# Cross-attention's sums by way of DRAM: one store, two loads and a wide reciprocal in place of ten transposes a pair

## The chip, the cores and the metric

One core of a Trainium2 chip. The metric is the device time of one execution in microseconds; the kernel before has a median of 562.46 us over three runs (562.35 to 567.57). The engines are TensorE (PE, with its weight loads as PEld), VectorE (DVE), ScalarE (ACT), GpSimd (POOL) and SyncE (SP), which issues nearly all DMAs.

## The reference

A decoder layer on x of (32, 64, 256), with context of the same shape. Each sublayer adds its result to x and is followed by a layer norm without gain.

```
x = layernorm(x + self_attention(x))          # 16 heads of 16, causal over 64 rows
x = layernorm(x + cross_attention(x, ctx))
x = layernorm(x + feed_forward(x))            # quantised 256 -> 1024 -> 256, silu, gelu, layer norm between
```

Cross-attention takes the 64 rows as channels and the 256 columns as positions: 8 heads of 8 channels.

```
q, k, v = heads(Wq x + bq), heads(Wk c + bk), heads(Wv c + bv)     # c: the context; q and k rotated
p   = softmax(q k^T / sqrt(8))                                     # 256 x 256 per head
out = Wo concat_heads(p v) + bo
```

## The kernel before

The 32 sequences are worked in 16 pairs; a pair's two sequences lie on 2 x 64 partitions. The first stage (`phase_a`) is a loop over bodies, -1 to 15. Body i works at once on several pairs: cross-attention's exponentials and products of pair i, the row maxima (`max_tile`) of the tiles 14 steps ahead, self-attention of pair i+3, and the end of cross-attention of pair i-1 (`prev`). Each engine runs a list written out by hand: a body has 16 steps `s`, and a line such as `if s == 13` says which piece stands after which step's tile. Engines meet by semaphores only. The maxima alternate between two PSUM banks, so TensorE's tile n waits for VectorE's reduction of tile n-2 (L574), and the exponentials do the same with ScalarE.

Cross-attention of a pair, per sequence b: `pv_quad` (L615) multiplies the exponentials by VA, whose 32 columns per head are 8 values and 24 ones. So u_b holds, on partition 32j + c and column 256 s4 + t, for c below 8 the weighted sum of value c of head 4 s4 + j at position t, and for c from 8 on copies of the sum of the exponentials. `u_copy` (L778) brings it to US of 128x512, after step 8 for b = 0 and after step 0 of the next body for b = 1. Then:

- `u_transpose` (L241): four 128x128 transposes on TensorE for each b, in step 13 and in step 3 of the next body;
- `u_norm` (L276): on VectorE a reciprocal of 16 sums a partition and a multiply, into AN;
- `att_transpose` (L250): two transposes back, in step 5; `at_copy` (L261) on ScalarE adds the value bias and writes AT;
- `x_out_proj` (L257) in step 9, `norm2_stats` (L291) in step 10, `rstd` on POOL, `norm2` in step 13.

SyncE's queue (`body` at L440) runs in order and each DMA waits for its data: `load_c`, `max_rows(i, 1)`, `cross_values`, `store_parts("q")`, `max_rows(nxt, 0)`, `expand_rows("q")`, `load_x`, `store_parts("k")`, `load_xT`, `expand_rows("k")`. `max_rows` (L405) puts the negated maxima into rows of QA, which the exponentials' product of steps 0 and 8 waits for; `expand_rows` (L379) reads the bf16 parts of q or k back from DRAM in copies.

A second program block follows: feed-forward in TURNS1 = 19 turns of the first product (`first_product`, `first_bias`), then 25 turns of the second stage. The last pair's end of cross-attention lies in its first turns: u_transpose ahead of turn 0, u_norm in turn 1, att_transpose in turn 2, x_out_proj in turn 3, norm2_stats in turn 4.

```
def max_ready(i, n):
    if has(i, 1) or n >= 2:
        pe.wait_ge(mx_red.sem, 16 * i.v + n - 1)
```

Of the kernel before, what the change touches and what calls it, by code (L numbers as in the profile page):

```python
# [80 lines left out]
def build_layer(nc, x, xT, ctx, wpT, woT, xW, xB, rows, w1T, w2T, attn_tables, rotary_tables, out):  # L81
    with ExitStack() as outer:
# [46 lines left out]
        RD = sb("RD", [P, 16])  # L129
        AN = sb("AN", [P, 2, 2, SEQ])  # L130
        AT = sb("AT", [P, D])
        Y2, st2, mv2, rs2 = sb("Y2", [P, D]), sb("st2", [P, 6]), sb("mv2", [P, 2]), sb("rs2", [P, 3])
# [4 lines left out]
        u_sb, ut_ps, u_nrm = event("u_sb", 2), event("ut_ps", 2), event("u_nrm", 4)  # L137
        at_ps, at_sb, xo_ps = event("at_ps"), event("at_sb"), event("xo_ps")
# [102 lines left out]
        def u_transpose(pe, i, b, ps):  # L241

            wait(pe, u_sb, i, b + 1)
            for u in range(2):
                for s4 in range(2):
                    q = 2 * u + s4
                    last = nc.tensor.transpose(ps[:, P * q:P * q + P], US[:, s4, P * u:P * u + P], ident)
            last.then_inc(ut_ps.sem, 1)

        def att_transpose(pe, i, ps):  # L250

            wait(pe, u_nrm, i, 4)
            for u in range(2):
                last = nc.tensor.transpose(ps[:, P * u:P * u + P], AN[:, u].rearrange("p b c -> p (b c)"), ident)
            last.then_inc(at_ps.sem, 1)

# [3 lines left out]

        def at_copy(act, i, g):  # L261
            wait(act, at_ps, i, 1)
            if has(i, 1):
                wait(act, xo_ps, i.plus(-1), 1)

            nc.scalar.activation(AT[:, :], g_b[g][:, 0:D], ACT.Identity, bias=xb["v"]).then_inc(at_sb.sem, 1)
# [9 lines left out]
        def u_norm(dve, i, b, g):  # L276
            wait(dve, ut_ps, i, b + 1)
            sums = g_b[g][:, :].rearrange("p (u h c) -> p u h c", u=2, c=32)
            if b == 1:
                wait(dve, u_nrm, i, 2)  # L280
            elif has(i, 1):
                wait(dve, u_nrm, i.plus(-1), 4)
                wait(dve, at_ps, i.plus(-1), 1)
            nc.vector.reciprocal(RD[:].rearrange("p (u h) -> p u h", u=2).unsqueeze(3),
                                 sums[:, :, :, XC:XC + 1]).then_inc(u_nrm.sem, 1)
            wait(dve, u_nrm, i, 2 * b + 1)
            nc.vector.tensor_tensor(AN[:, :, b, :].rearrange("p u (h c) -> p u h c", c=XC), sums[:, :, :, 0:XC],
                                    RD[:].rearrange("p (u h) -> p u h", u=2).unsqueeze(3).broadcast_to([P, 2, XH, XC]),
                                    ALU.mult).then_inc(u_nrm.sem, 1)

        def norm2_stats(dve, i, g):  # L291
            wait(dve, xo_ps, i, 1)
            if has(i, 1):
                wait(dve, ln2, i.plus(-1), 7)
            wait(dve, ln1, i, 7)
            nc.vector.scalar_tensor_tensor(out=Y2[:].unsqueeze(1), in0=g_b[g][:, 0:D].unsqueeze(1), scalar=xb["o"],
# [55 lines left out]
        def _(sp):  # L352
# [87 lines left out]
            def body(i):  # L440
                nxt, j, a = i.plus(1), i.plus(2), i.plus(3)
                if i.v >= 1 and real(a):
                    load_c(a)
                if real(i):
                    max_rows(i, 1)
                if real(a):
                    cross_values(a)
                if real(j):
                    store_parts("q", j)
                if real(nxt):  # L450
                    max_rows(nxt, 0)
                if real(j):
                    expand_rows("q", j)
# [9 lines left out]
                if real(a):  # L463
                    expand_rows("k", a)
# [841 lines left out]
        def _(dve):  # L1306
# [80 lines left out]
            for t in range(TURNS1):  # L1387
# [12 lines left out]
                if t == 9:  # L1400
                    factors(dve, 2)
# [71 lines left out]
```

## Time and profile before

| | |
|---|---|
| median of 3 runs | 562.46 us |
| the profiled execution | 563.8 us |
| its span, first to last instruction | 561.9 us |
| mean granted TensorE clock | 0.848 of full |
| busy: TensorE, VectorE, ScalarE, POOL | 450.6, 442.4, 382.0, 289.6 us |
| instructions | 12026 |

Times in the rows are microseconds from the span's start. "Busy" of an engine leaves out waits; a row's bracket gives the idle time before it and who ended it. A transfer's time to landing runs from its issue.

### The profile page before, as it was taken

What the parts mean: (1) busy time and instruction counts of PE and PEld (TensorE: products, weight loads), DVE (VectorE), ACT (ScalarE), POOL (GpSimd) and SP (SyncE); (2) the same over time, 40 slices, a digit from 0 to 9 for tenths busy, and PEclk for the clock granted to TensorE, in tenths of its full rate; (3) what the DMA queues carried; (4) which work ended last, traced back from release to release, by engine and by line L of the source; (5) the groups of instructions that cost most, each with busy time, mean ns of one, the idle gap of its engine ahead of it and who ended that gap; (6) DMA issues with size and microseconds to landing.
All of it is one profiled execution on the core that took longest, in us unless ns stands there. A gap on an engine that the chain in (4) does not pass through costs nothing. (4 is left out here: it accounts for less than half of the span.)

```text
span 561.9 us, 12026 instructions
## 1 busy us (share of the span) xinstructions
PE 450.6 (80%) x4162; PEld 243.0 (43%) x4162; DVE 442.4 (79%) x965; ACT 382.0 (68%) x698; POOL 289.6 (52%) x387
## 2 busy tenths in 40 slices
PE   6568799999999999999999999889877701555563
PEld 5354545555545555555555555433333200333342
DVE  2656687888988979889889798865848959999973
ACT  2222266767767667676676686687767787999972
POOL 5742565447555574475555744620032727667652
PEclk9677799999999999999999999975987875555555
DMA  6134318233242242332422323210000000000010
GB/s 217 48 97 149 97 46 248 66 92 91 57 111 67 64 110 60 90 91 60 108 69 64 106 61 82 71 56 1 3 1 1 1 0 1 10 28 19 30 37 29
DMA packets 51674, 37.07 MB, mean 66 GB/s; under 512 B 21408, under 2 KB 47648, under 8 KB 51488
## 3 DMA queue, kind: packets, MB, share of 16 engines
q1 hardware_dynamic: 51328, 36.10, 22.8%
q8 instruction: 33, 0.54, 0.4%
q10 hardware_dynamic: 288, 0.23, 0.2%
q14 instruction: 25, 0.20, 0.1%
HBM read 24.52 MB, written 10.49 MB: 62 GB/s over the span
## 5 line engine op out<-in xcount | busy, mean ns | idle before, releaser
L970 DVE TENSOR_REDUCE MX<-mx_b 128x2 f32<-128x512 f32 x256 | 167.8, 679 | 37.6 <-PE mx_b L581 36.4
L775 ACT ACTIVATE PB<-e_b 128x512 f32<-128x512 f32 x256 | 149.6, 592 | 64.7 <-PE e_b L609 63.8
L581 PE MATMUL mx_b<-KA,QA 48*128 48x256 bf16 x512 | 100.8, 282 | 10.3 <-DVE MX L970 10.1
L609 PE MATMUL e_b<-QA,KA 50*128 50x256 bf16 x512 | 100.9, 281 | 2.7 <-ACT PB L775 2.1
L626 PE MATMUL u_b<-PB,VA 128*32 128x256 f32 x1024 | 86.2, 404 | 3.4 <-ACT PB L775 2.9
L897 POOL TENSOR_TENSOR SP<-SP,srec 128x1024 f32<-128x1024 f32 x15 | 28.5, 1901 | 79.0 <-DVE srec L942 79.0
L581 PEld LDWEIGHTS mx_b<-KA,QA 48*128 48x128 bf16 x512 | 30.1, 95 | 88.5 <-issue 48.9
L1238 POOL TENSOR_TENSOR H<-H,row_tab 128x1024 f32<-128x1024 f32 x16 | 37.8, 2359 | 22.9 <-ACT H L1196 19.5
L1285 PE MATMUL r_b<-identh,Q 128*128 128x128 f16 x128 | 16.6, 311 | 39.5 <-ACT Q L1206 39.5
L1291 PE MATMUL z_b<-w2q,Q2T 128*128 128x256 bf16 x128 | 30.2, 417 | 19.3 <-ACT Q2T L1217 19.3
L314 POOL TENSOR_TENSOR rs<-mv,epsc 128x1 f32<-128x1 f32 x32 | 6.1, 189 | 72.5 <-DVE mv L301 50.2
L887 POOL TENSOR_TENSOR KM<-QK,att_tab 128x512 f32<-128x512 f32 x31 | 32.0, 1053 | 21.3 <-ACT QK L729 21.3
L486 PE MATMUL g_b<-XT,wp 128*128 128x128 f32 x256 | 34.5, 290 | 4.7 <-DMA wp<-in_wpT 4.7
L626 PEld LDWEIGHTS u_b<-PB,VA 128*32 128x32 f32 x1024 | 21.9, 109 | 33.5 <-issue 19.6
L486 PEld LDWEIGHTS g_b<-XT,wp 128*128 128x128 f32 x256 | 31.5, 200 | 7.9 <-DMA wp<-in_wpT 4.7
L754 ACT ACTIVATE PT<-g_b 128x512 f32<-128x512 f32 x32 | 17.6, 595 | 24.9 <-PE g_b L523 24.9
L609 PEld LDWEIGHTS e_b<-QA,KA 50*128 50x128 bf16 x512 | 29.1, 95 | 10.0 <-ACT PB L775 4.0
L1285 PEld LDWEIGHTS r_b<-identh,Q 128*128 128x128 f16 x128 | 12.5, 141 | 46.8 <-ACT Q L1206 46.7
L923 DVE TENSOR_REDUCE smax<-g_b 128x8 f32<-128x512 f32 x32 | 20.6, 686 | 12.0 <-PE g_b L510 12.0
L1291 PEld LDWEIGHTS z_b<-w2q,Q2T 128*128 128x128 bf16 x128 | 16.6, 140 | 29.5 <-ACT Q2T L1217 23.5
L1247 POOL TENSOR_TENSOR root<-base,halves 128x3 f32<-128x3 f32 x22 | 18.8, 852 | 19.2 <-DVE base L1374 10.2
L523 PE MATMUL g_b<-att_tab,SP 128*128 128x128 f32 x128 | 18.9, 297 | 8.8 <-POOL SP L897 4.7
(169 smaller groups left out, 1048.4 us busy)
## 6 DMA issues: line engine op xcount, KB each, us to landing
KA<-parts_k SPq DMA_DIRECT2D x64, 96.0 KB
QA<-parts_q SPq DMA_DIRECT2D x64, 96.0 KB
parts_q<-part_q SPq DMA_DIRECT2D x32, 128.0 KB, 2.0
parts_k<-part_k SPq DMA_DIRECT2D x16, 192.0 KB, 2.1
C<-in_ctx SPq DMA_DIRECT2D x16, 128.0 KB, 3.0
X<-in_x SPq DMA_DIRECT2D x16, 128.0 KB, 2.9
out_y<-O SPq DMA_DIRECT2D x16, 128.0 KB, 1.7
XT<-in_xT SPq DMA_DIRECT2D x15, 128.0 KB, 2.2
```

Source lines behind the costliest of these rows:

```text
L486: last = nc.tensor.matmul(ps[:, P * c:P * c + P], wp[:, k, P * c:P * c + P], XT[:, a.p, k, :], start=k == 0, stop=k == 1)
L581: m = nc.tensor.matmul(mx_b[n % 2][:, D * k:D * k + D], QA[low:low + K_MAX, 2 * i.ring + b, h, P * u:P * u + P], KA[low:low + K_MAX, 2 * i ...
L609: m = nc.tensor.matmul(e_b[n % 2][:, D * k:D * k + D], KA[low:low + K_EXP, 2 * i.ring + b, h, P * sc:P * sc + P], QA[low:low + K_EXP, 2 * ...
L626: last = nc.tensor.matmul(u_b[32 * j:32 * j + 32, D * s4:D * s4 + D], VA[:, i.p, sc, b, 4 * s4 + j, :], PB[:, (2 * m + j % 2) % 4, j // 2, :],
L775: nc.scalar.activation(PB[:, n % 4].rearrange("p e t -> p (e t)"), e_b[n % 2][:, :], ACT.Exp, scale=XC ** -0.5).then_inc(e_sb.sem, 1)
L887: ops.tensor_tensor(KM[:, c], QK[:, 2 + c, :].unsqueeze(1).broadcast_to([P, 4, P]), kmask.unsqueeze(2).broadcast_to([P, 4, P]), ALU.mult). ...
L897: ops.tensor_tensor(SP[:], SP[:], srec[:].unsqueeze(2).broadcast_to([P, SH, SEQ]), ALU.mult).then_inc(s_norm.sem, 1)
L923: nc.vector.tensor_reduce(smax[:].rearrange("p (c r k) -> p c r k", c=2, r=2)[:, :, r], g_b[r][:, :].rearrange("p (c k s) -> p c k s", c=2 ...
L970: nc.vector.tensor_reduce(MX[:, b, e, 2 * q:2 * q + 2, u], mx_b[n % 2][:, :].rearrange("p (e s) -> p e s", e=2), AXL.X, ALU.max).then_inc( ...
L1238: nc.gpsimd.tensor_tensor(H[:, i.v, :], H[:, i.v, :], gam, ALU.mult).then_inc(zg.sem, 1)
L1285: m = nc.tensor.transpose(r_b[j.p][:, P * k:P * k + P], low_half(Q2[:, j.p, P * k:P * k + P]), identh[:])
L1291: m = nc.tensor.matmul(z_b[j.p][:, 0:D], Q2T[:, j.p, k, :], w2q[:, k, :], start=k == 0, stop=k == 7)
```

## The change

US goes whole to a DRAM tensor u_hbm of (32 c, 4 j, 2 b, 512), one store for each b (`store_sums`, 256 KB). `load_sums` reads rows c = 8 to 15, copies of the sums, as RB, and rows c = 0 to 7, the values, as UV, both 128x256 with partition 16c + 4j + 2b + s4, so no transpose is needed. `reciprocals` on VectorE (step 6) inverts RB in place, `means` on POOL multiplies into AT, and `x_out_proj` uses Wo with its rows put in that order. The value bias is carried into the output bias once (`value_bias`). u_transpose, u_norm, att_transpose and at_copy are gone. For the last pair the load stands at the head of SyncE's list in the second block, reciprocals in turn 2, x_out_proj in turn 6, norm2_stats in turn 7, norm2_max in turn 10.

```diff
+        def store_sums(sp, i, b):
+            if has(i, 1):
+                sp.wait_ge(ld_uv, 16 * i.v)
+                sp.wait_ge(ld_us, 16 * i.v)
+            wait(sp, u_sb, i, b + 1)
+            sp.dma_start(u_hbm[:, :, b].rearrange("c j x -> j c x"), US[:].rearrange("p s t -> p (s t)")).then_inc(moved[b], 16)
+
+        def load_sums(sp, i):
+            if has(i, 1):
+                wait(sp, at_sb, i.plus(-1), 1)
+            for b in range(2):
+                sp.wait_ge(moved[b], 16 * (i.v + 1))
+            flat = u_hbm.rearrange("c j b x -> c (j b x)")
+            sp.dma_start(RB[:], flat[XC:2 * XC].rearrange("c (r t) -> (c r) t", t=D)).then_inc(ld_us, 16)
+            sp.dma_start(UV[:], flat[0:XC].rearrange("c (r t) -> (c r) t", t=D)).then_inc(ld_uv, 16)
+
+        def reciprocals(dve, i):
+            dve.wait_ge(ld_us, 16 * (i.v + 1))
+            nc.vector.reciprocal(RB[:], RB[:]).then_inc(u_rec.sem, 1)
+
+        def means(pool, i):
+            wait(pool, u_rec, i, 1)
+            pool.wait_ge(ld_uv, 16 * (i.v + 1))
+            if has(i, 1):
+                wait(pool, xo_ps, i.plus(-1), 1)
+            nc.gpsimd.tensor_tensor(AT[:], UV[:], RB[:], ALU.mult).then_inc(at_sb.sem, 1)
...
             def body(i):
-                nxt, j, a = i.plus(1), i.plus(2), i.plus(3)
+                prev, nxt, j, a = i.plus(-1), i.plus(1), i.plus(2), i.plus(3)
+                if real(prev):
+                    store_sums(sp, prev, 1)
+                if i.v >= 0 and real(j):
+                    expand_rows("k", j)
                 if i.v >= 1 and real(a):
                     load_c(a)
+                if real(prev):
+                    load_sums(sp, prev)
                 if real(i):
                     max_rows(i, 1)
                 if real(a):
                     cross_values(a)
                 if real(j):
                     store_parts("q", j)
+                if real(i):
+                    store_sums(sp, i, 0)
+                if real(j):
+                    expand_rows("q", j)
                 if real(nxt):
                     max_rows(nxt, 0)
-                if real(j):
-                    expand_rows("q", j)
...
-                if real(a):
-                    expand_rows("k", a)
...
-                    if s == 3 and real(prev):
-                        u_transpose(pe, prev, 1, use(g_b[2], u_nrm, prev, 4))
-                    if s == 5 and real(prev):
-                        att_transpose(pe, prev, use(g_b[2], at_sb, prev, 1))
-                    if s == 13 and real(i):
-                        u_transpose(pe, i, 0, use(g_b[1], u_nrm, i, 2))
+                    if s == 11 and i.v == 0:
+                        value_bias(1)
...
-                    if s == 3 and real(prev):
-                        u_norm(dve, prev, 1, 2)
+                    if s == 6 and real(prev):
+                        reciprocals(dve, prev)
-                    if s == 13 and real(i):
-                        u_norm(dve, i, 0, 1)
...
                 if real(j):
                     split_parts(pool, nc.gpsimd, "q", j)
+                if real(prev):
+                    means(pool, prev)
                 if real(a):
                     self_norm(pool, nc.gpsimd, a)
...
-                if t == 1:
-                    u_norm(dve, last, 1, 1)
+                if t == 2:
+                    reciprocals(dve, last)
                 if t == 4:
-                    norm2_stats(dve, last, 1)
                     factors(dve, 1)
                 if t == 7:
+                    norm2_stats(dve, last, 1)
+                if t == 10:
                     norm2_max(dve, last)
                     mean_square(dve, 2)
...
+            load_sums(sp, last)
```

VectorE in steps 3 to 9 of a full body, before (MX: maxima of cross-attention; smax, SP, ssum, srec: softmax of self-attention; RD, AN: u_norm):

```order
L970 TENSOR_REDUCE MX<-mx_b 128x2
L284 RECIPROCAL RD<-g_b 128x16
L287 TENSOR_TENSOR AN<-g_b,RD 128x2x64
L970 TENSOR_REDUCE MX<-mx_b 128x2
L923 TENSOR_REDUCE smax<-g_b 128x2x4 x2
L931 TENSOR_TENSOR SP<-g_b,smax 128x2x256
L970 TENSOR_REDUCE MX<-mx_b 128x2 x3
L931 TENSOR_TENSOR SP<-g_b,smax 128x2x256
L970 TENSOR_REDUCE MX<-mx_b 128x2 x2
L940 TENSOR_REDUCE ssum<-SP 128x16
```

The same steps in the changed kernel (RB: the copies of the sums):

```order
L974 TENSOR_REDUCE MX<-mx_b 128x2 x2
L927 TENSOR_REDUCE smax<-g_b 128x2x4 x2
L935 TENSOR_TENSOR SP<-g_b,smax 128x2x256
L974 TENSOR_REDUCE MX<-mx_b 128x2 x2
L277 RECIPROCAL RB<-RB 128x256
L974 TENSOR_REDUCE MX<-mx_b 128x2
L935 TENSOR_TENSOR SP<-g_b,smax 128x2x256
L974 TENSOR_REDUCE MX<-mx_b 128x2 x2
L944 TENSOR_REDUCE ssum<-SP 128x16
```

The pair RD, AN between the maxima of tiles 3 and 4 is gone; a reciprocal of 256 columns stands between those of tiles 6 and 7, ahead of the second subtraction and the self-attention sums.

SyncE from the KA loads to the parts of q, before (KA, QA: the operands of cross-attention; C: the context; MR: negated maxima; VM: values of self-attention):

```order
L392 DMA KA<-parts_k 24x1x2048 [waits stored_k0,e_ps]
L392 DMA KA<-parts_k 24x1x2048 x3
L368 DMA C<-in_ctx 128x256 [waits k_ps,xv_ps]
L408 DMA QA<-MR 2x8x128 [waits mt_sb]
L408 DMA QA<-MR 2x8x128
L402 DMA VM<-VS 64x8x16 [waits vs_sb,ao_ps]
```

The same place in the changed kernel:

```order
L264 DMA u_hbm<-US 4x32x512 [waits u_sb,ld_us,ld_uv]
L389 DMA KA<-parts_k 24x1x2048 [waits stored_k0,e_ps]
L389 DMA KA<-parts_k 24x1x2048 x3
L365 DMA C<-in_ctx 128x256 [waits k_ps,xv_ps]
L272 DMA RB<-u_hbm 128x256 [waits moved1,moved0,at_sb]
L273 DMA UV<-u_hbm 128x256
L405 DMA QA<-MR 2x8x128 [waits mt_sb]
L405 DMA QA<-MR 2x8x128
L399 DMA VM<-VS 64x8x16 [waits vs_sb,ao_ps]
```

A store of the sums now stands ahead of the KA loads, and two loads, which wait for both stores of the pair, ahead of the maxima's rows.

## Rows read from the trace of the kernel before

**Rows 1.** The page, part 2: TensorE's clock in 40 slices, tenths.
```profile
PEclk9677799999999999999999999975987875555555
```

**Rows 2.** Busy time over the loop's stretch; columns as the first line says.
```profile
core 0: us, PE busy (x) PEld busy (x) DVE busy (x) ACT busy (x) POOL busy (x), PEclk, DMA share, GB/s
79.00:405.00 326.00, 313.02 (x3290) 163.15 (x3288) 271.87 (x546) 234.57 (x495) 164.20 (x248) 0.97 0.29 79
```

**Rows 3.** The same view, the two halves of one full body.
```profile
254.37:266.57 12.20, 11.81 (x140) 6.32 (x137) 11.92 (x23) 8.92 (x18) 5.46 (x9) 1.00 0.21 48
266.57:276.86 10.29, 10.29 (x104) 5.68 (x108) 7.42 (x17) 7.29 (x17) 7.25 (x12) 1.00 0.41 121
```

**Rows 4.** Timeline of VectorE in that body: start, duration, instruction, idle before.
```profile
254.37 1.29 DVE L923 TENSOR_REDUCE smax<-g_b 128x8 f32<-128x512 f32 x2 [0.41 <-PE g_b L510]
...
256.18 1.88 DVE L970 TENSOR_REDUCE MX<-mx_b 128x2 f32<-128x512 f32 x3
...
261.05 0.25 DVE L942 RECIPROCAL srec<-ssum 128x16 f32<-128x16 f32 x1
...
266.92 0.69 DVE L970 TENSOR_REDUCE MX<-mx_b 128x2 f32<-128x512 f32 x1 [0.35 <-PE mx_b L581]
```

**Rows 5.** Timeline of TensorE in that body.
```profile
252.08 0.65 PE L247 MATMUL g_b<-att_tab,US 128*128 128x128 f32 x4
...
256.91 0.28 PE L581 MATMUL mx_b<-KA,QA 48*128 48x256 bf16 x1 [0.36 <-DVE MX L970]
...
265.29 0.66 PE L247 MATMUL g_b<-att_tab,US 128*128 128x128 f32 x4
265.87 0.69 PE L536 MATMUL g_b<-PT,VM 128*32 128x64 f32 x32
```

**Rows 6.** Timeline of POOL and of ScalarE in that body.
```profile
261.38 1.90 POOL L897 TENSOR_TENSOR SP<-SP,srec 128x1024 f32<-128x1024 f32 x1 [5.47 <-DVE srec L942]
...
264.06 1.09 ACT L754 ACTIVATE PT<-g_b 128x512 f32<-128x512 f32 x2 [0.85 <-PE g_b L523]
```

**Rows 7.** Groups of VectorE by shape: count, busy us, mean ns, idle before.
```profile
L284 DVE RECIPROCAL RD<-g_b 128x16 f32<-128x16 f32 x32 | 8.0, 249 | 3.7 <-PE g_b L247 3.7
L942 DVE RECIPROCAL srec<-ssum 128x16 f32<-128x16 f32 x16 | 4.0, 253 | 0.6
L1339 DVE RECIPROCAL sc<-sc 128x1 f32<-128x1 f32 x16 | 2.6, 160 | 0.1
...
L949 DVE TENSOR_TENSOR Y<-g_b,X 128x256 f32<-128x256 f32 x16 | 6.8, 425 | 13.7 <-PE g_b L545 13.6
```

**Rows 8.** Timeline around SyncE's KA loads; DMA issues with landing; a POOL row.
```profile
270.22 0.59 ACT L784 ACTIVATE US<-u_b 128x512 f32<-128x512 f32 x1
271.45 2.78 SPq L392 DMA_DIRECT2D KA<-parts_k  x4
...
C<-in_ctx SPq DMA_DIRECT2D x16, 128.0 KB, 3.0
parts_k<-part_k SPq DMA_DIRECT2D x16, 192.0 KB, 2.1
...
265.36 0.73 POOL L905 TENSOR_TENSOR full_k<-rot_k 128x256 f32<-128x256 f32 x1
```

**Rows 9.** Busy time and clock near the loop's end.
```profile
340.60:362.40 21.80, 19.45 (x219) 9.48 (x219) 19.30 (x39) 15.02 (x34) 12.34 (x19) 1.00 0.26 72
370.00:375.00 5.00, 2.53 (x26) 0.85 (x29) 2.84 (x7) 4.78 (x10) 1.00 (x3) 0.86 0.04 8
```

**Rows 10.** Timeline of body 15 and of the second block's start.
```profile
402.81 0.60 ACT L784 ACTIVATE US<-u_b 128x512 f32<-128x512 f32 x1
408.12 0.75 PE L609 MATMUL e_b<-QA,KA 50*128 50x256 bf16 x4
416.93 0.60 ACT L784 ACTIVATE US<-u_b 128x512 f32<-128x512 f32 x1 [0.36 <-PE u_b L626]
422.15 1.28 DVE L1317 SCALAR_TENSOR_TENSOR YB<-f_b,deq,row_tab 128x1024 f32<-128x1024 f32 x1 [1.94 <-PE f_b L1276]
424.50 1.28 DVE L1317 SCALAR_TENSOR_TENSOR YB<-f_b,deq,row_tab 128x1024 f32<-128x1024 f32 x1 [0.80 <-PE f_b L1276]
```

More of the change, by code:

```diff
@@ L136, in build_layer @@
         ln1 = event("ln1", 7)
-        u_sb, ut_ps, u_nrm = event("u_sb", 2), event("ut_ps", 2), event("u_nrm", 4)
-        at_ps, at_sb, xo_ps = event("at_ps"), event("at_sb"), event("xo_ps")
+        u_sb, u_rec = event("u_sb", 2), event("u_rec")
+        at_sb, xo_ps = event("at_sb"), event("xo_ps")
+        s_bias_ps, s_bias = sem("s_bias_ps"), sem("s_bias")
+        u_hbm = nc.dram_tensor("u_hbm", (32, 4, 2, 2 * D), F32, kind="Internal").ap()
+        moved, ld_uv, ld_us = [sem(f"moved{b}") for b in range(2)], sem("ld_uv"), sem("ld_us")
         ln2 = event("ln2", 7)
@@ L238, in tile_at @@
             return i.plus(n // 16), n % 16
[L241 to L255, printed above, removed]
         def x_out_proj(pe, i, ps):
@@ L259, in x_out_proj @@
             nc.tensor.matmul(ps[:, 0:D], xw["o"], AT[:, :], start=True, stop=True).then_inc(xo_ps.sem, 1)
[L261 to L266, printed above, removed]
         def square_sum(act, i):
@@ L780, in u_copy @@
                 if b == 1:
[L781 removed]
+                    act.wait_ge(moved[0], 16 * (i.v + 1))
                 elif has(i, 1):
[L783 removed]
+                    act.wait_ge(moved[1], 16 * i.v)
                 nc.scalar.activation(US[:].rearrange("p s t -> p (s t)"), u_b[:, :], ACT.Copy).then_inc(u_sb.sem, 1)
@@ L850, in body @@
                         mt_copy(i, 1, 0)
-                    if s == 5 and real(prev):
-                        at_copy(act, prev, 2)
                     if s == 7 and real(nxt):
@@ L995, in _ @@
             dve.wait_ge(ld_att, 16)
-            nc.vector.tensor_tensor(identb[:].rearrange("p (b t) -> p b t", b=2),
-                                    ident[:, 0:HALF].unsqueeze(1).broadcast_to([P, 2, HALF]),
-                                    ident[:, HALF:P].unsqueeze(1).broadcast_to([P, 2, HALF]), ALU.add).then_inc(s_tab, 1)
+            for r in range(2):
+                own = slice(HALF * r, HALF * r + HALF)
+                nc.vector.tensor_copy(identb[own, :].rearrange("p (b t) -> p b t", b=2),
+                                      ident[own, own].unsqueeze(1).broadcast_to([HALF, 2, HALF])).then_inc(s_tab, 1)
             nc.vector.tensor_copy(maskb[:], mask.unsqueeze(1).broadcast_to([P, 8, SEQ])).then_inc(s_tab, 1)
@@ L1029, in body @@
                         norm2_stats(dve, prev, 1)
-                    if s == 13 and real(i):
-                        u_norm(dve, i, 0, 1)
+                    if s == 11 and i.v == 0:
+                        value_bias()
                     if s == 14 and real(prev):
@@ L1221, in _ @@
                 first_values(t)
-                if t == 1:
-                    at_copy(act, last, 0)
-                if t == 5:
+                if t == 8:
                     norm2(act, last)
@@ L1251, in _ @@
             mean_power(pool, 1)
+            means(pool, last)
             rstd(pool, ln2, last, mv2, rs2)
-            mean_power(pool, 2)
             for n in range(NPAIR):
+                if n == 5:
+                    mean_power(pool, 2)
                 wait(pool, qb, Pair(0, n), 1)
@@ L1292, in second_product @@
                 m.then_inc(z_ps.sem, 1)
-            pe.wait_ge(s_tab, 3)
-            u_transpose(pe, last, 1, g_b[1])
+            pe.wait_ge(s_tab, 4)
             for t in range(TURNS1):
-                if t == 2:
-                    att_transpose(pe, last, g_b[0])
-                if t == 3:
+                if t == 6:
                     x_out_proj(pe, last, g_b[1])
```

48 lines of the change are left out of this document (22 added, 26 removed).

## The prediction, made before the changed kernel ran

> **What bounds the kernel now.** I read the busy shares by slice first, then the sums over stretches, then the order of instructions of one loop body on each engine, and last the waits. The slices show one long plateau at full TensorE clock and a second stage at lower clock [rows 1]. The plateau is the loop over pairs, 0 to 15: TensorE is busy for 313.0 of its 326 us, VectorE for 271.9 [rows 2]. A mean over it hides that a body has two halves. Take the body of the trace from 254.37 to 276.86 (22.49 us; the twelve full bodies, pairs 1 to 12, repeat it). In the first 12.20 us VectorE is busy for 11.92 and TensorE queues behind it; in the other 10.29 us TensorE is busy for 10.29 and VectorE for 7.42 only [rows 3]. VectorE's own rows say the same: from the row maxima at 254.37 nothing there waits until 266.92, where it waits 0.35 us for TensorE [rows 4]; TensorE at 256.91 waits for VectorE's maximum [rows 5]. So work that leaves TensorE pays in the second half, and work that is added to VectorE costs in the first.
>
> The first half ends on a chain: reciprocal of the self-attention sums (ends 261.30), POOL's scaling (to 263.28), four and four transposes, ScalarE's copies (264.06 to 265.15), then on TensorE the first u_transpose at 265.29, the self-attention product at 265.87, and the maxima of tile 14, for which VectorE waits [rows 4 to 6].
>
> **What goes.** Per pair: two u_transpose groups on TensorE, one in step 13 and one in step 3; the row starts of the first are 0.58 us apart from the product behind it (265.29 to 265.87), and the second has the same length, 0.65 against 0.66 us [rows 5]. att_transpose in step 5 goes too, but there TensorE waits for VectorE soon after (256.91), so I cost it at nothing: the maximum reductions hide it, and it would be worth at most 0.4 us a body (a group half as long). VectorE loses two pairs of reciprocal (0.25) and multiply (about 0.3): 0.54 us in step 13 and 0.54 in step 3. Step 3 is in TensorE's half, where VectorE idles. The one in step 13 stands behind the last maximum of the first half, parallel to the chain above, and lets VectorE follow the earlier TensorE. at_copy leaves ScalarE, which limits nothing here: nothing.
>
> **What comes on VectorE.** One reciprocal of 128x256 in step 6, in the middle of the busy half. No row has that size. One column takes 160 ns, 16 columns from PSUM 249 and from SBUF 253 [rows 7]: (253 - 160) / 15 = 6.2 ns a column, while an ordinary 128x256 pass takes 425 ns in all. At 6.1 to 6.2 a column it is 0.16 + 255 x 0.0061 = 1.72 us at the lower end. Bounds: 0.43 us, if it ran like the one-pass row, and 2.0 us, if the slope over few columns flatters it (a quarter more). I take 1.72, since both 16-column rows lie on that slope.
>
> The Trainium skill ("VectorE: DVE Perf Modes", First, the fixed hardware budget) says that Reciprocal runs as an iterated divide with a repeat count of 8; at its 0.96 GHz that would be an estimated 2.1 us, and the sum below would rise by 12 x 0.4 = 5 us. At that clock the rows' slope is about 6 cycles, so the trace agrees with an iterated divide but not with eight.
>
> **How it meets the chain.** The reciprocal follows the maximum of tile 6, which ends near 257.45 (two of the three in the row at 256.18). Tile 7's maximum, the second subtraction, ScalarE's second exponential, the sums and their reciprocal all move by 1.72, since VectorE never idles between: sums' reciprocal to 263.02, POOL to 265.0, ScalarE's copies to 266.87, product at 267.0, since without the u_transpose it follows the copies after 0.14 us and not after 0.72. Tile 14's maximum, about 1.05 us behind the product as before, starts at 268.05 instead of 266.92: +1.1 us [rows 4 to 6]. TensorE's half then loses the 0.58 us of step 3. Per full body 1.1 - 0.58 = +0.5, twelve bodies: +6.2 us.
>
> **The round trip to DRAM.** It is hidden if the copies of the sums land before step 6. ScalarE's copy of the second half of the sums ends at 270.81; SyncE then issues the store (0.45 us), the four KA loads, which already stood at 271.45 to 274.2, and load_c; the load of the sums' copies follows at 274.75, when the store (256 KB; 192 KB lands in 2.1 us) has long landed. 128 KB loads land in up to 3.0 us [rows 8], so at 277.7. Step 6 of that body is at 257.45 + 22.49 - 0.58 = 279.4: 1.7 us to spare. POOL's product of 128x256 takes 0.73 us [rows 8], ends at about 281.9, and the output projection of step 9 comes at about 282.8. It lies in POOL's idle time before the self-attention scaling. Behind the load's wait stand max_rows, cross_values and store_parts: max_rows moves by 0.9 us for two more issues, and its result is wanted only in step 8, some 5 us later. max_rows of the next pair moves behind the QA loads (2.8 us) and still has half a body. I cost all of this at nothing; without the cover each microsecond late costs one a body.
>
> **The ends.** Body 0 loses one u_transpose and gains a one-column product and add: -0.5. Bodies 13 and 14 have no self-attention; TensorE is at half clock for much of 370 to 394 [rows 1, 9], where each group is worth double, and VectorE waits for it, so most of the reciprocal hides: -2.0 for both, from -4 to 0. Body 15 is short: the sums' second half is copied at 402.81 to 403.4, store landed 405.8, two loads issued to 406.8, then max_rows, landed about 409.4, where the exponentials' product of tile 8 wanted it at 408.12 [rows 10]: +1.2. Last, pair 15: its copy ends at 417.53; store, landing, load, landing take 0.1 + 2.3 + 2.4 to 3 us, to 422.4; VectorE now waits for it in turn 2, ahead of the first bias, which stood at 422.15 [rows 10]. With 1.72 us of reciprocal and one quantisation the bias starts near 424.5, +2.3; some 1.0 comes back, because TensorE is then two tiles ahead and later waits for it (0.80 at the next bias) vanish: +1.3.
>
> Sum: 6.2 - 0.5 - 2.0 + 1.2 + 1.3 = +6.2 us, on the profiled execution of 563.8 us (span 561.9). That execution is 1.3 us over the median of 562.46; the difference carried to the median gives 568.6 us.
>
> **Rivals.**
> *The reciprocal is cheap.* At the one-pass price of 0.43 us the first half changes by 0.43 - 0.6 and the second by -0.58: -0.75 a body, -9 for twelve, the ends -1.5: 552 us. It decides as soon as the reciprocal is under 1.2 us, the two groups' sum. For it: TensorE's busy share. Against: the slope of rows 7. Chance 0.08.
> *Two columns at a time.* From SBUF to SBUF half of the columns might go beside the other half: 0.16 + 127 x 0.0061 = 0.94 us, so a body gains 0.26 and the total is about -4: 558 us. The row from SBUF (253) is no quicker than the one from PSUM (249), which speaks against it. The skill's rule for it is "VectorE: DVE Perf Modes", Mode 2x_2P: a single-source fp32 operation within SBUF gets both ports; the two rows don't show it for this operation. Chance 0.10.
> *The copies come late.* Store, KA loads and load share the queues; if the sums land 1 us after step 6 wants them, VectorE's busy half grows by that: 12 us more, 581 us. Against it stand the 1.7 us. Chance 0.12.
> *The clock falls.* TensorE gets gaps of about 1 us by step 9. It held full clock with 19.45 of 21.80 us busy and lost it around a stretch of 2.53 of 5 [rows 9]; the new bodies would have about 20 of 23. If it falls in the bodies, each grows by several us: 600 us and more. Chance 0.04.
> *The gain of TensorE counts more*, that is att_transpose counts with 0.3 and the ends cost nothing: 12 x 0.2 + 0 = +2: 565 us. Chance 0.21.
>
> **Numbers.** The forecast has 0.45. About 1% is what a measurement can tell from no change. Faster by more (below 556.8): the first rival and part of the second, 0.14. Within: the rest of that, the last rival and the forecast's lower part, 0.36. Slower: 0.50. The range of 8 in 10 is 556 to 579: it leaves out the cheap reciprocal, the clock and half of the late copies. The forecast's own range is 564 to 574 (reciprocal 1.6 to 2.0, ends +-2).
>
> **What would show it.** In the profile after: a reciprocal row of 128x256 at 1.7 us; period of a full body 23.0; VectorE without a gap from the row maxima to tile 13 for about 13 us; TensorE waiting for the maxima in step 9 by 1 us; no wait of VectorE for the sums' load except in bodies 15 and in turn 2. The forecast is wrong if the reciprocal row is under 1.2 us, if VectorE waits for the load in every body, or if the period is below 22.5.

## The result, and the profile of the changed kernel

| | before | changed |
|---|---|---|
| median | 564.62 us (562.35 to 567.57, 4 runs) | 625.44 us (622.84 to 627.55, 4 runs) |
| ratio | | 1.107, 95% interval 1.099 to 1.115 |
| profiled execution (span) | 563.8 us (561.9) | 624.59 us (622.4) |
| start of body 1 (ScalarE copies the sums) | 89.03 us | 90.07 us |
| bodies 1 to 13 | 292.7 us | 339.6 us |
| body 14 | 21.1 us | 21.3 us |
| body 15 | 14.1 us | 22.3 us |
| last copy of the sums to the first bias of block 2 | 5.2 us | 10.4 us |

The forecast was 568.6 us. Medians here and below are over all executions of a kernel; the ratios leave out those more than 1.5% above the kernel's fastest, such as the profiled one of the idle stores with 4 outermost (609.59 us), whose rows show the kind of wait and not its price. A body runs here from its step 0 copy of the sums to the next (before, bodies 14 and 15 start at 381.74 and 402.81). Of the 60.5 us of span, the bodies 1 to 13 hold 46.9, body 15 8.2, the start of block 2 5.2, all else 0.2.

The chain of waits of the changed kernel, its line sums and four of its longest pieces (start, length, what):

```profile
by line: DMA u_hbm<-US 15.8%; issue 8.6%; DMA QA<-MR 6.5%; DMA RB<-u_hbm 6.0%; DVE RB L277 3.9%; SPq L389 3.3%; PE u_b L630 3.2%; DVE sth L1366 2.9%; PE mx_b L585 2.7%; DVE sc L1390 2.5%; DVE H L1332 2.4%; DVE MX L974 2.1%; ACT PB L781 2.0%
...
137.02 5.31 DMA QA<-MR
...
300.42 7.18 DMA u_hbm<-US
307.67 2.50 DMA RB<-u_hbm
326.62 7.14 DMA u_hbm<-US
```

In body after body the chain runs through the store of the sums, over 7 us from its issue to its landing, and then through the load. The rows of MR in it (137.02) are those for the next pair, issued behind the store of the pair's first sequence. SyncE's timeline in one full body, against [rows 8]:

```profile
300.42 0.58 SPq L264 DMA_DIRECT2D u_hbm<-US  x1
301.09 2.81 SPq L389 DMA_DIRECT2D KA<-parts_k  x4
304.00 0.42 SPq L365 DMA_DIRECT2D C<-in_ctx  x1
307.67 0.33 SPq L272 DMA_DIRECT2D RB<-u_hbm  x1
308.05 0.42 SPq L273 DMA_DIRECT2D UV<-u_hbm  x1
308.53 1.16 SPq L405 DMA_DIRECT2D QA<-MR  x2
```

The order is the forecast's. But SyncE stands from 304.42 to 307.67 for the store, and behind it stand the rows of MR, which TensorE wants. The waits, and VectorE's first row behind the load:

```profile
DVE RB L277 <- DMA RB<-u_hbm: 30.9, 15, 5.8
...
PE e_b L613 <- DMA QA<-MR: 28.5, 23, 4.5
```
```profile
310.19 1.75 DVE L277 RECIPROCAL RB<-RB 128x256 f32<-128x256 f32 x1 [0.88 <-DMA RB<-u_hbm]
```
```profile
C<-in_ctx SPq DMA_DIRECT2D x16, 128.0 KB, 5.9
X<-in_x SPq DMA_DIRECT2D x16, 128.0 KB, 4.8
RB<-u_hbm SPq DMA_DIRECT2D x16, 128.0 KB, 2.5
```

The context's load, which nobody changed, lands in 5.9 us instead of the 3.0 of [rows 8]. What the DMA engines did while the store ran beside the KA loads, and, for comparison, the kernel before at its KA and C loads:

```profile
DMA packets 75, 0.18 MB, mean 51 GB/s; under 512 B 2, under 2 KB 2, under 8 KB 75
...
q1 hardware_dynamic: 75, 0.18, 29.1%
```
```profile
DMA packets 393, 0.63 MB, mean 124 GB/s; under 512 B 72, under 2 KB 297, under 8 KB 393
```

(first: 301.5 to 305 of the changed kernel; then 271.45 to 276.5 of the kernel before.) The share of 29.1% is over 16 engines: on the mean between four and five of them were at work. The sixteen were far from full. A clearer row is body 15, where the same store runs alone. First 454.5 to 456.9 of the changed kernel, then 438.5 to 439.9 of the kernel that stores the same 256 KB with 128 outermost (in the experiments below, 604.64 us); the first line of each is the share of the 16 engines in tenths, in 40 slices:

```profile
DMA  1240410106121112222222222222222222222121
...
q1 hardware_dynamic: 104, 0.21, 24.9%
```
```profile
DMA  0000000455979496996979697933000000000000
...
q1 hardware_dynamic: 144, 0.26, 48.4%
```

With 4 outermost the share settles at 24.9%, that is four of sixteen, and the store lands after 6.3 us; with 128 it reaches 9 tenths, and the store lands after 2.0. The Trainium skill has the rule ("DMA: Bandwidth & Descriptors", Why a DMA increments its semaphore by 16 and not by 1): a transfer is spread over the largest number of engines up to 16 that divides both sides' slowest dimension, and on these queues it takes the lowest-numbered. The store's DRAM side is 4 x 32 x 512, so four. The share of 24.9% and the late neighbours agree with it; no row here numbers the engines.

VectorE's new row and the clock, against [rows 7] and [rows 1, 2]:

```profile
L277 DVE RECIPROCAL RB<-RB 128x256 f32<-128x256 f32 x16 | 28.0, 1753 | 30.9 <-DMA RB<-u_hbm 30.9
...
PEclk9578998989889797897978979886775696555555
```
```profile
79.00:430.00 351.00, 304.78 (x2996) 158.60 (x2996) 266.75 (x475) 211.88 (x451) 173.06 (x258) 0.89 0.37 103
299.74:325.95 26.21, 23.78 (x234) 12.68 (x231) 19.97 (x36) 15.60 (x35) 12.97 (x20) 0.87 0.34 96
```

In a body of 26.21 us no engine is full: TensorE 23.78, VectorE 19.97. The granted clock has holes in the loop that were not there before (0.87 in this body, 1.00 in the kernel before's), so that part of TensorE's own work got longer too.

### The profile page after: what moved, and what is told of

It reads as the page before. It is cut to its first block, busy times and chain, and to the rows that moved or that the text cites. A ratio compares the mean times of both kernels' runs of the same rounds, so it can differ in the third digit from the quotient of the medians.

```text
span 622.4 us, 11699 instructions
## 1 busy us (share of the span) xinstructions
PE 462.1 (74%) x4004; PEld 242.5 (39%) x4004; DVE 458.4 (74%) x919; ACT 375.7 (60%) x682; POOL 301.2 (48%) x403
## 4 chain that ended last, share of the span: by engine, by line
DMA 30%; DVE 24%; PE 18%; issue 9%; ACT 7%; SPq 6%; POOL 6%; ACTq 0%; POOLq 0%; DVEq 0%
DMA u_hbm<-US 16%; DMA QA<-MR 6%; DMA RB<-u_hbm 6%; DVE RB L277 4%; SPq L389 3%; PE u_b L630 3%; DVE sth L1366 3%; PE mx_b L585 3%; DVE sc L1390 2%; DVE H L1332 2%; DVE MX L974 2%; ACT PB L781 2%; DVE YB L1325 2%; ACT US L790 2%; PE g_b L562 2%
## 5 line engine op out<-in xcount | busy, mean ns | idle before, releaser
L781 ACT ACTIVATE PB<-e_b 128x512 f32<-128x512 f32 x256 | 146.5, 592 | 77.4 <-PE e_b L613 76.4
L613 PE MATMUL e_b<-QA,KA 50*128 50x256 bf16 x512 | 102.7, 300 | 32.0 <-DMA QA<-MR 28.5
L585 PE MATMUL mx_b<-KA,QA 48*128 48x256 bf16 x512 | 105.0, 295 | 15.8 <-DVE MX L974 15.3
L630 PE MATMUL u_b<-PB,VA 128*32 128x256 f32 x1024 | 96.0, 436 | 11.5 <-ACT PB L781 11.2
L585 PEld LDWEIGHTS mx_b<-KA,QA 48*128 48x128 bf16 x512 | 34.6, 97 | 96.1 <-DVE MX L974 53.3
L284 POOL TENSOR_TENSOR AT<-UV,RB 128x256 f32<-128x256 f32 x16 | 12.5, 779 | 92.4 <-DVE RB L277 92.4
L901 POOL TENSOR_TENSOR SP<-SP,srec 128x1024 f32<-128x1024 f32 x15 | 28.5, 1902 | 50.1 <-DVE srec L946 50.1
L277 DVE RECIPROCAL RB<-RB 128x256 f32<-128x256 f32 x16 | 28.0, 1753 | 30.9 <-DMA RB<-u_hbm 30.9
L613 PEld LDWEIGHTS e_b<-QA,KA 50*128 50x128 bf16 x512 | 31.9, 97 | 46.8 <-DMA QA<-MR 33.4
L753 ACT ACTIVATE SP<-SP 128x512 f32<-128x512 f32 x32 | 19.7, 625 | 39.8 <-DVE SP L935 39.8
L630 PEld LDWEIGHTS u_b<-PB,VA 128*32 128x32 f32 x1024 | 25.1, 115 | 43.8 <-ACT PB L781 27.5
L760 ACT ACTIVATE PT<-g_b 128x512 f32<-128x512 f32 x32 | 17.7, 595 | 23.7 <-PE g_b L527 23.7
```

What stands on the lines that cost most here:

```text
L277: nc.vector.reciprocal(RB[:], RB[:]).then_inc(u_rec.sem, 1)
L585: m = nc.tensor.matmul(mx_b[n % 2][:, D * k:D * k + D], QA[low:low + K_MAX, 2 * i.ring + b, h, P * u:P * u + P], KA[low:low + K_MAX, 2 * i ...
L613: m = nc.tensor.matmul(e_b[n % 2][:, D * k:D * k + D], KA[low:low + K_EXP, 2 * i.ring + b, h, P * sc:P * sc + P], QA[low:low + K_EXP, 2 * ...
L630: last = nc.tensor.matmul(u_b[32 * j:32 * j + 32, D * s4:D * s4 + D], VA[:, i.p, sc, b, 4 * s4 + j, :], PB[:, (2 * m + j % 2) % 4, j // 2, :],
L781: nc.scalar.activation(PB[:, n % 4].rearrange("p e t -> p (e t)"), e_b[n % 2][:, :], ACT.Exp, scale=XC ** -0.5).then_inc(e_sb.sem, 1)
L901: ops.tensor_tensor(SP[:], SP[:], srec[:].unsqueeze(2).broadcast_to([P, SH, SEQ]), ALU.mult).then_inc(s_norm.sem, 1)
```

## The experiments

Each ratio is to the kernel before on the same chip in the same hours (its medians 563.2, 565.2, 564.7, 563.5 and 563.5 us for the five groups). "No trip" below means: no store and no loads of the sums, the means' inputs are constants, and the output lacks cross-attention's means.

### What does the arithmetic cost, what the trip?

**No trip, reciprocal kept.** Store and loads deleted, `RB` and `UV` filled with ones:

```
-                if real(prev):
-                    store_sums(sp, prev, 1)
...
-                if real(prev):
-                    load_sums(sp, prev)
```

> The changed kernel without the trip to DRAM: no store of the sums, no loads, RB and UV are filled with ones once, reciprocal and product run on them as before, so the output lacks cross-attention's means. Theory A: the whole excess over my sum is the trip; what stays is the reciprocal in VectorE's busy half less the two transpose groups, so 562 to 570 us (bodies +6, body 0 and bodies 13 to 15 -2.5). Rival C (the reciprocal at its place disturbs TensorE's clock and the self-attention chain more than its length): 590 us or more, with full-body period above 24.5 us.

568.13 us, ratio 1.003 (0.998 to 1.008), a body 22.87. All but a few us of the loss is the trip, as theory A had it.

**Reciprocal alone**, added to the kernel before at step 6, on tiles of its own:

```
+                    if s == 6 and real(prev):
+                        nc.vector.reciprocal(RY[:], RX[:])
```

> The kernel before, with one more instruction a body: a reciprocal of 128x256 on VectorE in step 6, on a tile of ones that nobody else reads; the output is the reference's. Theory A (VectorE's first half is a bound): each body of 1 to 12 grows by nearly the whole 1.75 us, together +18 to +23 us, 580 to 586 us, period 24.1 to 24.2. Rival D (slack in VectorE or TensorE's queue takes it up): under +8 us, 563 to 570 us. Rival C (the gap drops the clock): over +35 us.

578.32 us, ratio 1.023 (1.013 to 1.033), a body 24.02: 1.53 of the instruction's 1.75 us show. The total is a little under the 580 to 586 expected, because body 13 took 19.4 us at a granted clock of 1.00 where the kernel before had 22.0 at 0.82.

**No trip, no reciprocal.**

> No store, no loads (the means' inputs are constants) and no reciprocal on VectorE; GpSimd's multiplication, the output product and the second norm stay. Leaves out the means of cross-attention. It prices what the removal of the transposes, copies and small divisions alone gives. Theory A (VectorE bounds one half, TensorE the other; the reciprocal's 1.75 us cost 1.53 us a body beside the kernel before): against the no-trip kernel's 568.13 and 22.87 us a body, 1.5 us less a body, 21.3 to 21.5, and 545 to 551 in all. Rival (a body of 22.5 us is bound by TensorE or by a loop of waits and not by VectorE's work): 22.3 or more, 560 to 565.

551.85 us, ratio 0.975 (0.966 to 0.983), a body 21.34. So the removed operations give 22.49 - 21.34 = 1.15 us a body and the reciprocal takes back 22.87 - 21.34 = 1.53.

### Is it the order in SyncE's queue?

**Rows of MR ahead of the loads** (`max_rows(i, 1)` now stands before `load_sums(sp, prev)`):

> The changed kernel with one swap in SyncE's list: max_rows(i, 1) stands ahead of load_sums, so that the maxima's rows no longer wait behind the loads that wait for the slow store. If the blocked queue is the larger part of the loss (theory A1), the matmuls' wait for the maxima's rows falls from 28.5 us to under 10, and the time falls to 595 to 612 us. If the slow store itself and the late copies are (theory A2), VectorE's wait for the copies only grows by the 1.2 us of two issues and the time stays within 1.5% of 625 us.

628.39 us, ratio 1.113 (1.104 to 1.122). TensorE's wait for the rows fell from 28.5 to 18.1 us and VectorE's for RB from 30.9 to 24.0, and nothing was won. The rows have two places. Those for step 8, which were moved, cost 4.6 us of waits in place of 22.3. But those for the next pair stand behind the store of the pair's first sequence, land 5.2 us after their issue, and their waits rose from 6.2 to 13.5 us. So it isn't one place in the queue: both stores are slow, and both hold up what follows them.

### Is it the shape of the store?

**Four stores of 32 rows:**

```
-            sp.dma_start(u_hbm[:, :, b].rearrange("c j x -> j c x"), US[:]...).then_inc(moved[b], 16)
+            for j in range(4):
+                sp.dma_start(u_hbm[:, j, b], US[32 * j:32 * j + 32]...).then_inc(moved[b], 16)
```

> The whole store of the sums is cut into four, one for each 32 partitions, same bytes, same place in SyncE's list. Theory A (the store's shape): the one transfer, written as 4 x 32 rows, runs on 4 of the 16 DMA engines, lands 6 us after its issue and holds up SyncE and the other transfers on those engines. Then four transfers of 32 rows land in about 2.5 us, SyncE's wait for the store (52.6 us in all) falls under 10 us, the matmuls' wait for the maxima's rows (28.5 us) and VectorE's wait for the copies of the sums (30.9 us) mostly vanish, and the time falls to 568 to 580 us. Rival B (too many bytes, or DRAM writes as such): the same 256 KB take as long in four pieces, SyncE issues longer, and the time stays at 615 to 635 us.

590.39 us, ratio 1.041 (1.029 to 1.054), above the 568 to 580 expected; most bodies 22.9 to 23.4. A piece lands in 1.7 us, the context in 3.1. TensorE's wait for the rows is 5.9 us, VectorE's for RB 10.0.

**One store of 128 rows.** Only the DRAM tensor's order and the matching order of the weights change:

```
-        u_hbm = nc.dram_tensor("u_hbm", (32, 4, 2, 2 * D), ...)
+        u_hbm = nc.dram_tensor("u_hbm", (4, 32, 2, 2 * D), ...)
...
-            sp.dma_start(u_hbm[:, :, b].rearrange("c j x -> j c x"), ...)
+            sp.dma_start(u_hbm[:, :, b].rearrange("j c x -> (j c) x"), ...)
```

> The changed kernel with the DRAM tensor laid out 4 x 32 x 2 x 512 in place of 32 x 4 x 2 x 512, so that one store of the sums has 128 rows as its outermost dimension on both sides; still one store of 256 KB and two loads of 128 KB, same bytes, same packets of 2 KB, same waits. The loads' outermost dimension on the DRAM side is now 4 where it was 8. Theory A (a transfer's outermost dimension decides over how many of the 16 DMA engines it is spread; 4 made the store slow, 5.8 to 6.3 us to the loads' issue): the store is done about 2.5 to 3.1 us after its issue (as the four pieces of 32 rows), the loads take longer than their 2.5 us (3 to 4), and the time falls to 585 to 600, near the 590.39 of the store in four pieces. Theory B (the bytes or the 2 KB packets written to DRAM are slow, and four separate transfers help because they are four): the one store still takes 5.8 us and the time stays at 620 to 630.

604.64 us, ratio 1.071 (1.061 to 1.081), a little above what theory A gave. The trace of one of its full bodies has the store's landing; the waits show where the rest went:

```profile
u_hbm<-US SPq DMA_DIRECT2D x1, 256.0 KB, 2.4
```
```profile
PE e_b L614 <- DMA QA<-MR: 24.7, 14, 4.2
DVE RB L278 <- DMA RB<-u_hbm: 17.4, 14, 4.4
```

One transfer, the same 256 KB in the same 2 KB packets: 2.4 us. Theory B (bytes, packets, or the number of transfers) is out. But now the loads have 4 as their outermost dimension in DRAM.

**The store by itself, in the kernel before.** Two stores a body of a constant tile, for which nothing waits but the next such store, once into 32 x 4 x 2 x 512 and once into 4 x 32 x 2 x 512:

```
+            sp.dma_start(x_hbm[:, :, b].rearrange("c j x -> j c x"), EX[:]).then_inc(s_ex[b], 16)
```

> The kernel before, with two more stores a body of a constant 128 x 512 tile into a DRAM tensor of 32 x 4 x 2 x 512, where the changed kernel has its stores and in its shape (outermost dimension 4 in DRAM); nothing but the next such store waits for them. It prices what the store takes from the others' transfers, apart from the chain through the sums. Theory A1 (part of the loss is that the store holds engines which the loads of KA, C, X and the rows of MR need too): C's landing goes from 3.0 to 5 us or more, TensorE waits for QA<-MR some 5 to 20 us in all, and the time is 570 to 585. Rival A2 (the store costs only those that wait for it): C may land later but nobody waits, 563 to 567.

> The same two idle stores a body in the kernel before, into a DRAM tensor of 4 x 32 x 2 x 512, 128 rows outermost on both sides: same bytes and packets. Theory A: C's landing stays under 4 us, TensorE waits for QA<-MR under 3 us in all, 563 to 568, less than the idle stores with 4 outermost by what those cost. Theory B (bytes to DRAM are what hurts): as slow as those, within 0.5%.

602.12 us, ratio 1.060 (1.049 to 1.071), with 4 outermost; 568.15 us, ratio 1.004 (1.001 to 1.008), with 128 outermost. Theory A1 held and its price was set too low: by the ratios some 31 us lie between two kernels that move the same bytes in the same packets. Bodies of the first take 23.7 to 27.0 us, those of the second the 22.49 of the kernel before. First the waits and landing with 4 outermost, then with 128:

```profile
DVE MX L984 <- PE mx_b L595: 78.5, 89, 3.3
...
PE e_b L623 <- DMA QA<-MR: 20.3, 13, 2.6
```
```profile
C<-in_ctx SPq DMA_DIRECT2D x16, 128.0 KB, 6.5
```
```profile
DVE MX L984 <- PE mx_b L595: 39.6, 52, 3.0
...
PE e_b L623 <- DMA QA<-MR: 0.7, 1, 0.7
```
```profile
x_hbm<-EX SPq DMA_DIRECT2D x31, 256.0 KB, 2.9
...
C<-in_ctx SPq DMA_DIRECT2D x16, 128.0 KB, 4.0
```

So much of the loss needs nobody that waits for the sums: the rows of MR (two transfers of 4 KB) come late beside the store. That they queue behind it on engines that both use is inferred from this, not seen.

**The loads of the 128-row kernel in four pieces each:**

> The kernel with the store in 128 rows (604.64), each of its two loads in four pieces of 32 rows, so that no transfer of the sums has an outermost dimension of 4; six SyncE issues more a body ahead of the rows of MR. Theory A (the loads with 4 outermost hold engines that the rows of MR need, 24.7 us of TensorE's waits): the loads land in under 3 us, the wait for the rows of MR falls under 15 us though they are issued some 2.5 us later, 585 to 600. Rival (what costs is the place of the rows in SyncE's queue, not the loads' engines): the wait for the rows of MR grows, 605 to 625.

612.00 us, ratio 1.088 (1.081 to 1.094). A piece lands in 2.0 us, but TensorE waits 30.5 us for the rows, issued behind six issues more. The rival's number came out, but theory A's mechanism is in the trace as well. The later transfer of MR's rows, issue and time to landing, first behind the two whole loads, then behind their eight pieces:

```profile
298.76 4.08 DMA QA<-MR
```
```profile
284.89 1.63 DMA QA<-MR
```

From issue to landing they take 4.1 us in the one and 1.6 in the other (3.8 to 4.6 and 1.6 in the bodies of the two chains of waits). But they are issued 9.7 us into the body instead of 6.1, so the six issues cost more than the pieces gave. Place in the queue and the loads' few engines both count; this run doesn't separate them.

### Can the trip be taken off the path?

In all of these the second norm ends one body later, so that nobody is near to waiting for the sums.

**Late reciprocal and means** (steps 11 and 12; loads behind the rows of MR), and the second one without the trip:

> The kernel with the store in 128 rows (604.64), with the same computation and output, in which nobody is near to waiting for the sums: the two loads are issued behind the rows of MR and cross-attention's values, the reciprocal stands at step 11, the means behind the self-attention's division, the output product at step 13, the second norm's statistics at step 14, its scaling and maximum in the next body. Theory A (what is left of the loss is the wait for RB, 17.4 us in 14 waits, the wait for the rows of MR, 24.7 us in 14, of which the loads with 4 outermost hold the engines, and the reciprocal's place): no wait for RB is left, that for MR under 5 us, body 22.0 to 22.8, 560 to 575. Rival (any traffic through DRAM of this size costs the other transfers whatever its place): 590 or more, with the wait for MR over 15 us.

> As the kernel with late loads, the reciprocal at step 12, the output product at step 14, the second norm's statistics at step 15. Theory A: the reciprocal lies wholly in the half that TensorE bounds, body 21.3 to 22.3, 552 to 568, a version that may beat the kernel before. Rival (the second norm's statistics now hold the bank that the first norm's product wants, and the next pair's queries come late): 0.3 us or more a body above the kernel with step 11.

> The no-trip kernel (no store and no loads of the sums, reciprocal of 128x256 kept on constants; leaves out the means of cross-attention) with the reciprocal moved out of VectorE's full half of the body: reciprocal at step 12 in place of 6, means after the self-attention's division on GpSimd, output product at step 14, the second norm's statistics at step 15, its scaling at step 2 and its maximum at step 3 of the next body (of body 15's own, at its end). Theory A (the reciprocal costs 1.53 us a body only because VectorE bounds the half in which it stands; in the other VectorE has some 2.9 us free): 22.87 us a body falls to 21.3 to 22.0, and 568.13 to 550 to 560. Rival (the body is elastic, VectorE's total counts wherever the instruction stands): 22.7 or more, 565 to 570.

633.50, 636.02 and 630.51 us (ratios 1.120, 1.124 and 1.115): a miss of mine, and without the trip as bad as with it. GpSimd of the last one:

```profile
270.29 0.72 POOL L286 TENSOR_TENSOR AT<-UV,RB 128x256 f32<-128x256 f32 x1 [2.72 <-DVE RB L280]
274.60 0.19 POOL L313 TENSOR_TENSOR rs<-mv,epsc 128x1 f32<-128x1 f32 x1 [3.58 <-DVE mv L300]
...
275.74 0.73 POOL L906 TENSOR_TENSOR full_k<-rot_k 128x256 f32<-128x256 f32 x1
```

The split of the keys had been left behind the means and the second norm on GpSimd's queue. Its first instruction (275.74) starts 0.3 us before the next body (copy at 275.99), without the move 4.6 us before (271.20 against 275.81), and ScalarE's wait for the first norm's power behind it went from 13.0 to 49.3 us in 15 waits. Of the trip the first of the three says one thing: behind it TensorE waits once for the rows of MR, 0.9 us, and VectorE twice for RB, 6.4 us in all.

**GpSimd's keys first, the rest in the next body's steps 3 to 7:**

> The no-trip kernel (568.13; leaves out the means of cross-attention) with the reciprocal at step 12, and this time nothing that the next pair waits for behind it: GpSimd splits the keys first and takes the means last, the output product and the second norm's statistics stand at step 3 of the next body (bank 2, where the transposes stood), its scaling at step 6 and its maximum at step 7. Theory A (the reciprocal costs only where VectorE bounds; the 630.51 of the kernel with later means came from GpSimd's order, the keys' split queued behind the second norm's power, 4.0 us of ScalarE's wait for it a body): a body of 21.3 to 22.0, 550 to 560. Rival (VectorE's total counts wherever the reciprocal stands): 22.7 or more, 565 to 570.

> The same order of work with the sums' real way through DRAM: store in 128 rows, loads issued behind the rows of MR and cross-attention's values; computes everything. Theory A (with a quick store and the loads off the path nothing of the trip is left but its SyncE issues): within 6 us of the kernel without the trip in this order, 552 to 566, a version that can beat the kernel before. Rival (the trip's traffic costs the other transfers even then): over 575, with waits of TensorE for the rows of MR over 10 us.

571.19 us (1.013, 1.008 to 1.018) without and 580.27 us (1.028, 1.022 to 1.034) with the trip. Full bodies are 22.45 us in both: the trip, stored in 128 rows and off the path, costs a full body nothing (one in twelve takes 23.6). Of the 9 us between the two, 7.3 lie behind body 15, where nothing covers store and loads. Theory A's times were missed in both: without the trip the rival's number came out, and with it the time is over the rival's 575, but TensorE waits only once for the rows of MR, 0.8 us. But output product and statistics had moved into TensorE's half as well, so one more pair moved the reciprocal alone (to step 13; product, statistics, scaling and maximum keep steps 9, 10, 13, 14 and serve the pair before):

> The no-trip kernel (568.13, 22.87 us a body; leaves out the means of cross-attention) in which output product, the second norm's statistics, scaling and maximum keep their steps (9, 10, 13, 14) but work on the pair before, and only the reciprocal changes its half of the body (step 13 in place of 6), the means last on GpSimd; in body 15 the last two pairs are served at other steps. Theory A (VectorE is the bound of one half and has 2.9 us free in the other; the kernel with everything behind stayed at 22.45 because the output product and the statistics had moved into TensorE's half with the reciprocal): a body of 21.3 to 21.9, near the 21.34 without a reciprocal, 553 to 562. Rival (the half in which the reciprocal stands does not matter beyond 0.4 us, since VectorE's work moves over from one half to the other): 22.3 to 22.5, 565 to 571.

> The same order with the sums' real way through DRAM (store in 128 rows, loads behind the rows of MR and cross-attention's values); computes everything. Theory A: full bodies as long as without the trip, 21.3 to 21.9, and with body 15 and the second block's start, where nothing covers store and loads, 6 to 10 us on top: 558 to 570, within 1% of the kernel before. Rival (in shorter bodies the trip's loads meet the rows of MR again): bodies of 22.5 or more, over 575.

Without the trip 559.26 us (0.992, 0.988 to 0.997), a body 21.70: of the reciprocal's 1.53 us in step 6, 0.36 are left in step 13. It is the half of the body it stands in, not VectorE's total, that sets what it costs. With the trip, computing everything, 572.14 us (1.016, 1.013 to 1.020), over the 558 to 570 expected: most bodies at 21.7 to 22.1, others up to 23.7. Against the same order without the trip, body 15 starts 9.4 us later, and 5.4 us more are lost behind it. At the copy that starts body 15 it is level with the kernel before (402.41 against 402.81), and body 15 loses 6.1 us. Body 15 in four kernels (before, no trip, no trip and no reciprocal, this one):

```profile
402.81:416.93 14.12, 11.85 (x110) 4.33 (x106) 6.91 (x19) 10.89 (x24) 4.55 (x4) 1.00 0.01 2
```
```profile
411.05:425.30 14.25, 9.98 (x100) 3.03 (x96) 7.57 (x15) 10.41 (x22) 5.13 (x5) 0.94 0.01 2
```
```profile
390.39:410.32 19.93, 15.37 (x100) 3.84 (x96) 5.89 (x14) 10.49 (x22) 4.56 (x4) 0.50 0.00 1
```
```profile
402.40:422.60 20.20, 15.98 (x102) 4.15 (x98) 9.15 (x20) 11.57 (x25) 6.18 (x8) 0.52 0.12 41
```

Body 15 takes 14 us at a granted clock of 0.94 to 1.00 (2.4 GHz) and 20 at 0.50 (1.2 GHz), with no trip and no reciprocal in it too. In the last kernel it also ends two pairs and not one, so that not all of its 20.20 us need be the clock's; without the trip it takes 20.19, at 0.52 too. No version here beats the kernel before with the whole computation.

## Why the prediction was wrong, point by point

- **The failed step: "I cost all of this at nothing", the round trip.** It rested on "the store (256 KB; 192 KB lands in 2.1 us) has long landed" by 274.75, 3.9 us after the copy of the sums. The landing was taken over from a transfer of another shape (the parts of k) by its size. Measured: 7.1 to 7.4 us in most full bodies, and 5.7 and 6.3 us where it runs alone (issued 473.96 and 451.66). That turned the 1.7 us to spare into a wait of VectorE for RB 15 times, for 16 pairs. Of the 57 us that the trip costs (625.44 against 568.13), the store's shape alone holds some 35 (590.39 in four pieces); the rest was not split up. The shape stood in the diff and in the order's row (4x32x512); I read the bytes only. Nor did the step ask what the store does to others: the idle stores price that alone at some 31 us. "max_rows of the next pair ... still has half a body" failed with it: behind the store of the first sequence these rows land 5.0 to 6.1 us after their issue, and TensorE waits for them nine times, 6.2 us in all.
- **The rival "the copies come late"** was the right mechanism at a chance of 0.12 and a fifth of its size: 581 us is 12 us over the forecast, for copies 1 us late, and 57 were measured. It left out the rows of MR behind the load's wait, which I had named and given 5 us of room.
- **The reciprocal: right.** 1.72 us forecast, 1.753 measured; the slope of [rows 7] holds out to 256 columns. The estimates made from the Trainium skill ("VectorE: DVE Perf Modes"), 2.1 us from the repeat count of 8 (First, the fixed hardware budget) and 0.94 from both ports (Mode 2×_2P) at the slope of the rows, are both off for it. The upper bound was added up wrongly: a quarter more slope gives 2.1 us, not 2.0; nothing hung on it.
- **The body without the trip: right in sum, both terms short.** Forecast +0.5, measured +0.38 = 1.53 - 1.15. The reciprocal at +1.1 passed on 1.53, as [rows 3] would have said (VectorE 11.92 of 12.20 busy); the removed operations at -0.58 gave 1.15, which is near 0.58 and VectorE's 0.54 us in step 13 together; which of them counted was not tried apart.
- **The ends.** Body 0 and its neighbours -0.5 forecast, +1.0 measured; bodies 13 and 14 -2.0 forecast, +2.6 and +0.2 measured; body 15 +1.2 forecast, +8.2 measured: TensorE waits 4.53 us for the rows of MR and VectorE 5.6 for RB, store issued 451.66, load 458.01, and the granted clock is 0.67 in it instead of 1.00. The start of block 2 +1.3 forecast, +5.2 measured:

```profile
481.85 1.75 DVE L277 RECIPROCAL RB<-RB 128x256 f32<-128x256 f32 x1 [5.85 <-DMA RB<-u_hbm]
...
483.69 1.28 DVE L1325 SCALAR_TENSOR_TENSOR YB<-f_b,deq,row_tab 128x1024 f32<-128x1024 f32 x1
```

- **The clock.** The rival's price was for a fall by itself. It came as a consequence of the waits: 0.89 over the loop against 0.97 [rows 2]. How much of the 46.9 us it holds was not separated from the waits.

## What to carry to other kernels

Read the landing of a transfer from a row with its own shape, not its size: write down the outermost dimension of both sides, and put one there that 16 divides (here 128 or 32 in place of 4). Ask of each new transfer what stands behind its wait on its queue and which small transfers share its engines; an idle copy in the kernel before, in the shape planned, prices that in one run. And an instruction costs by the half of the loop it stands in, so price it there, and see what a move puts behind it on every queue.

## What I had not expected of the hardware

- One store of 256 KB in 2 KB packets: 7.2 us (5.7 and 6.3 alone, at a steady 24.9% of the 16 engines) with 4 outermost in DRAM, 2.0 to 2.9 us with 128 outermost, and some 31 us of a kernel between the two when nobody waits for it.
- Neighbours suffer though most engines are free: a 128 KB load beside it 5.9 to 6.5 us instead of 3.0, at a share of 29.1% of the engines; and 4 KB behind two loads with 4 outermost 4.1 us instead of the 1.6 behind the same loads in pieces of 32 rows.
- A reciprocal of fp32 on VectorE costs the same per column at 16 and at 256 columns: 253 and 1753 ns, 6.2 ns for each column over the 160 of the first.
- The clock behind the loop is part of the price, and it isn't told by the length of the bodies: body 15 ran at 1.00 in the kernel before (bodies of 22.49 us), at 0.50 in the one without trip and reciprocal (21.34), 14.1 against 19.9 us, and at 0.50 too in the one without the trip and everything behind (22.45, the 571.19 us). In both the clock had fallen to 0.50 in body 14 already. With the reciprocal alone (24.02) it stayed at 1.00 in body 13, where the kernel before had 0.82. What decides it was not tried.
